# One load queue in the order x, x2, adj, and float32 products for one and a half units, in a two-branch graph layer

## The reference

```python
def _cxin_conv(x, a, eps, W, b):            # N = 4096, D = 128, L = 3
    ax = a @ x
    h = ax + (1.0 + eps[0]) * ax
    for i in range(L):
        h = jax.nn.relu(h @ W[i].T + b[i])
    return h

h = jnp.maximum(_layernorm(x, axis=-1), 0.0)         # eps 1e-05
out1 = _cxin_conv(h,  adj, eps1, W1, b1)
out2 = _cxin_conv(x2, adj, eps2, W2, b2)
return x + jnp.concatenate((out1, out2), axis=1) @ Wm.T + bm
```

## Time and profile before

| | us |
|---|---|
| median of 3 runs | 406.74 (406.16 to 407.13) |
| profiled execution, own time | 406.39 |
| its span | 404.7 |
| PE busy | 400.2 (99%) |
| PEld busy | 325.4 (80%) |
| DVE busy | 219.1 (54%) |
| ACT busy | 219.4 (54%) |
| POOL busy | 30.5 (8%) |
| DMA | 76.21 MB, mean 188 GB/s |

### The profile page before, as it was taken

One profiled execution on the slowest core, in us unless ns is written; L12 is line 12 of the kernel. 1 busy time (PEld: TensorE's weight loads), 2 busy tenths in 40 slices (PEclk: granted clock), 3 DMA queues, 4 the chain that ended last, 5 costly groups with the idle time before them and its releaser, 6 DMA issues.

```text
span 404.7 us, 4822 instructions
## 1 busy us (share of the span) xinstructions
PE 400.2 (99%) x1751; PEld 325.4 (80%) x1751; DVE 219.1 (54%) x258; ACT 219.4 (54%) x259; POOL 30.5 (8%) x35
## 2 busy tenths in 40 slices
PE   8999999999999999999999999999999999999997
PEld 2788888888888888888888888888888888888886
DVE  3998887656464434551645517345373444755223
ACT  4877667657564533555433556334565335766034
POOL 0243332100010000000100001000000000000100
DMA  7997786754636165334574336653175550740100
GB/s 303 420 377 285 296 314 238 244 208 160 232 146 210 44 241 205 109 120 191 186 280 164 122 128 236 230 206 141 67 262 204 207 196 38 275 166 2 52 0 28
DMA packets 14029, 76.21 MB, mean 188 GB/s; under 512 B 1920, under 2 KB 2176, under 8 KB 6080
## 3 DMA queue, kind: packets, MB, share of 16 engines
q1 hardware_dynamic: 12240, 71.18, 46.9%
q0 software_dynamic: 1200, 3.93, 2.9%
q10 hardware_dynamic: 576, 0.92, 0.6%
HBM read 73.93 MB, written 2.10 MB: 188 GB/s over the span
## 4 chain that ended last, share of the span: by engine, by line
PE 97%; DMA 2%; ACTq 0%; DVE 0%; issue 0%; DVEq 0%
PE acc L591 24%; PE acc L588 24%; PE acc L587 24%; PE second_acc L587 3%; PE second_acc L591 3%; PE second_acc L588 3%; PE hidden L588 3%; PE hidden L591 3%; PE hidden L587 3%; PE acc L605 2%; PE second_acc L605 2%; DMA adj_raw<-adj_first 2%; PE second_acc L619 1%; PE merged L588 1%; PE merged L591 1%; PE merged L587 1%
## 5 line engine op out<-in xcount | busy, mean ns | idle before, releaser
L588 PE MATMUL acc<-adj_hi,feat_hi 128*128 128x512 f32 x432 | 168.1, 389 | 0.0
L587 PE MATMUL acc<-adj_hi,feat_lo 128*128 128x512 f32 x432 | 168.1, 389 | 0.0
L591 PE MATMUL acc<-adj_lo,feat_hi 128*128 128x512 f32 x432 | 168.0, 389 | 0.0
L447 DVE TENSOR_TENSOR adj_lo<-adj_raw,adj_hi 128x2048 fp32r<-128x2048 f32 x48 | 108.3, 2289 | 36.7 <-ACT adj_hi L277 35.8
L277 ACT ACTIVATE adj_hi<-adj_raw 128x2048 fp32r<-128x2048 f32 x48 | 90.3, 1925 | 16.5 <-PE acc L591 14.6
L453 DVE TENSOR_TENSOR act_lo<-act_f,act_hi 128x512 fp32r<-128x512 f32 x60 | 41.0, 690 | 105.3 <-ACT act_f L297 105.3
L588 PEld LDWEIGHTS acc<-adj_hi,feat_hi 128*128 128x128 f32 x432 | 81.1, 188 | 17.1
L587 PEld LDWEIGHTS acc<-adj_hi,feat_lo 128*128 128x128 f32 x432 | 81.1, 188 | 17.1
L591 PEld LDWEIGHTS acc<-adj_lo,feat_hi 128*128 128x128 f32 x432 | 81.1, 188 | 16.8
L296 ACT ACTIVATE act_hi<-hidden,bias 128x512 fp32r<-128x512 f32 x45 | 30.9, 687 | 96.2 <-PE hidden L591 96.2
L507 DVE TENSOR_TENSOR adj_lo<-adj_raw,adj_hi 128x2048 fp32r<-128x2048 f32 x14 | 31.5, 2289 | 6.5 <-ACT adj_hi L315 6.2
(11 more groups left out here) (91 smaller groups left out, 251.3 us busy)
## 6 DMA issues: line engine op xcount, KB each, us to landing
adj_raw<-adj_tiles SPq DMA_DIRECT2D x62, 1024.0 KB, 5.1
x_rows<-x_tiles SPq DMA_DIRECT2D x15, 256.0 KB, 7.1
x_res<-x_t POOLq DMA_DIRECT2D x8, 256.0 KB, 6.4
out_t<-y_sb POOLq DMA_DIRECT2D x7, 256.0 KB, 2.3
adj_raw<-adj_second SPq DMA_DIRECT2D x2, 512.0 KB, 6.6
adj_raw<-adj_first ACTq DMA_DIRECT2D x2, 256.0 KB, 5.0
adj_raw<-adj_first SPq DMA_DIRECT2D x2, 256.0 KB, 4.7
w_raw<-w_t SPq DMA_DIRECT2D x1, 512.0 KB, 5.8
```

Of the source, the lines that this page charges most:

```text
L447: nc.vector.tensor_tensor(adj_lo[:, u % RING, :], adj_raw[:, u % RING, :], f32(adj_hi[:, u % RING, :]), ALU.subtract).then_inc(lo_made, 1)
L587: nc.tensor.matmul(out, lhs_lo, rhs_hi, start=start, stop=False)
L588: nc.tensor.matmul(out, lhs_hi, rhs_hi, start=False, stop=False)
L591: return nc.tensor.matmul(out, lhs_hi, rhs_lo, start=False, stop=stop)
```

## The change

- SP's queue issues x, x2, then all pieces of both first units, then the rest as before. ACT issues no loads any more.
- `WARM_UP` is 12 instead of 8.
- `raw_aggregate` is done for the first unit and for the first half of the second. The other half of the second unit goes through three float32r passes in branch 1, at the end of a new `opening_of_second`. The branch-0 products of the two units are now done one unit after the other (`opening_of_first`, `opening_of_second`).
- The sixteen subtractions that make `feat_lo` move from GpSimd to DVE, each to a written-out place in DVE's order. GpSimd's program now begins with its load of `x_res`.
- Epsilon is added in the root as its bias, a constant tile `ln_eps`; the Newton step reads variance and epsilon in one operation. One small DVE operation per tile goes.
- The order of ACT's work in the opening changes with it; the tile of x2 with u = 0 is rounded early, not after the second tile.

```diff
-    WARM_UP = 8
+    WARM_UP = 12
...
-
+            load_x(0)
             load_x2(0)
-            for s, i in ((0, 1), (0, 2), (1, 0), (1, 1)):
+            for s, i in [(s, i) for s in range(len(PIECES)) for i in range(len(PIECES[s]))]:
                 to, piece_of, done = piece_load(s, i)
                 sp.dma_start(to, piece_of).then_inc(done, 16)
...
         @block.gpsimd
         def _(pool):
 
-            def low_of_x2(u):
...
-            low_of_x(0)
-            for u in range(1, U):
-                low_of_x2(u)
-                low_of_x(u)
-                if u == 1:
-                    low_of_x2(0)
             pool.dma_start(x_res[:, :], x_t[:, 0:CW]).then_inc(res_loaded, 16)
...
-                nc.scalar.activation(std[:, :], var_eps[:, :], ACT.Sqrt).then_inc(std_made, 1)
+                nc.scalar.activation(std[:, :], mean_var[:, :, 1], ACT.Sqrt, bias=ln_eps[:, :]).then_inc(std_made, 1)
...
-            for i in (0, 3):
-                if i == 3:
-                    act.dma_start(x_rows[:, 0], x_tiles[0]).then_inc(x_loaded[0], 16)
-                to, piece_of, done = piece_load(0, i)
-                act.dma_start(to, piece_of).then_inc(done, 16)
-            act.wait_ge(zero_made, 1)
+            act.wait_ge(constants_made, 2)
             nc.scalar.activation(root_of_zero[:, :], zero[:, :], ACT.Sqrt)
 
-            for i in range(len(PIECES[0]) - 1):
-                piece_high(0, i)
+            piece_high(0, 0)
             std_of_x(0)
-            piece_high(0, len(PIECES[0]) - 1)
-            piece_high(1, 0)
+            piece_high(0, 1)
+            high_of_x2(0)
             act.wait_ge(rstd_made, 1)
             rectify_half(0, half_relu_made, half_feat1_made)
+            piece_high(0, 2)
+            piece_high(0, 3)
+            rectify_half(1, relu_made, feat1_hi_made)
+            piece_high(1, 0)
             piece_high(1, 1)
-            rectify_half(1, relu_made, feat1_hi_made)
             high_of_x2(1)
-            high_of_half(2, 0)
             std_of_x(1)
-            high_of_half(2, 1)
+            high_of_opening(2)
             high_of_opening(3)
...
-                step(last)
-                nc.vector.tensor_scalar(var_eps[:, :], mean_var[:, :, 1], LN_EPS, None, ALU.add).then_inc(var_made, 1)
+                last.then_inc(var_made, 1)
...
+            def low_of_x2(u):
+                rows = slice(u * JB, (u + 1) * JB)
+                dve.wait_ge(x2_loaded[u % X_SLOTS], 16 * (u // X_SLOTS + 1))
+                dve.wait_ge(feat2_hi_made, u + 1)
+                nc.vector.tensor_tensor(feat_lo[:, 1, rows, :], x2_rows[:, u % X_SLOTS], f32(feat_hi[:, 1, rows, :]),
+                                        ALU.subtract).then_inc(feat2_lo_made, 1)
...
             variances(0)
             scale_and_shift(0)
-            for i in range(2, len(PIECES[0])):
-                piece_low(0, i)
-            for i in range(len(PIECES[1])):
-                piece_low(1, i)
+            piece_low(0, 0)
+            piece_low(0, 1)
+            low_of_x2(0)
+            piece_low(0, 2)
+            piece_low(0, 3)
             variances(1)
+            low_of_x(0)
+            piece_low(1, 0)
+            piece_low(1, 1)
+            low_of_x2(1)
             scale_and_shift(1)
             low_of_opening(2)
             low_of_opening(3)
+            low_of_x(1)
             for u in range(2, U - 2):
                 variances(u)
                 scale_and_shift(u)
+                low_of_x2(u)
                 low_of_opening(2 * u)
                 low_of_opening(2 * u + 1)
+                low_of_x(u)
...
+            def opening_of_first():
+
+                out = opening_bank(0, late)
+                pe.wait_ge(half_feat1_made, 1)
+                pe.wait_ge(fine_hi_made, HALF)
+                passes(out, 0, late, [(feat_hi, adj_hi)], range(HALF), start=True)
+                pe.wait_ge(fine_lo_made, HALF)
+                passes(out, 0, late, [(feat_hi, adj_lo)], range(HALF))
+                pe.wait_ge(feat1_hi_made, 1)
+                pe.wait_ge(hi_made, 1)
+                passes(out, 0, late, [(feat_hi, adj_hi)], range(HALF, JB))
+                pe.wait_ge(lo_made, 1)
+                passes(out, 0, late, [(feat_hi, adj_lo)], range(HALF, JB))
                 pe.wait_ge(feat1_lo_made, 1)
-                for s in range(2):
-                    signal(0, late, passes(opening_bank(s, late), s, late, [(feat_lo, adj_hi)]))
+                signal(0, late, passes(out, 0, late, [(feat_lo, adj_hi)]))
+
+            def opening_of_second():
+
+                halves = range(HALF), range(HALF, JB)
+                out = opening_bank(1, late)
+                pe.wait_ge(fine_hi_made, len(PIECES[0]))
+                passes(out, 1, late, [(feat_hi, adj_hi)], halves[0], start=True)
+                pe.wait_ge(fine_lo_made, len(PIECES[0]))
+                passes(out, 1, late, [(feat_hi, adj_lo)], halves[0])
+                pe.wait_ge(hi_made, 2)
+                passes(out, 1, late, [(feat_hi, adj_hi)], halves[1])
+                passes(out, 1, late, [(feat_lo, adj_hi)])
+                pe.wait_ge(lo_made, 2)
+                passes(out, 1, late, [(feat_hi, adj_lo)], halves[1])
+                pe.wait_ge(feat2_hi_made, 1)
+                pe.wait_ge(feat2_lo_made, 1)
+                signal(0, late, passes(opening_bank(1, first), 1, first,
+                                       [(feat_hi, adj_hi), (feat_lo, adj_hi), (feat_hi, adj_lo)], halves[1]))
...
-            for at in range(len(PIECES)):
-                raw_aggregate(at)
-            norm_aggregate()
+            raw_aggregate(0, range(len(PIECES[0])))
+            raw_aggregate(1, [0])
+            opening_of_first()
+            opening_of_second()
```

More of the change, by code:

```diff
@@ L106, in gnn_layer_kernel @@
         zero = sb("zero", [P, 1])
+        ln_eps = sb("ln_eps", [P, 1])
         act_f = sb("act_f", [P, 2, CW])
@@ L134, in gnn_layer_kernel @@
         fine_lo_made = sem("fine_lo_made")
-        zero_made = sem("zero_made")
+        constants_made = sem("constants_made")
         unit_used = sem("unit_used")
@@ L474, in variances @@
                     last = nc.vector.bn_aggr(mean_var[:, j, :], stats[:, j, :])
-                step(last)
-                nc.vector.tensor_scalar(var_eps[:, :], mean_var[:, :, 1], LN_EPS, None, ALU.add).then_inc(var_made, 1)
+                last.then_inc(var_made, 1)
             def scale_and_shift(u):
                 r0, nt = rstd0[:, :], newton[:, :]
+                dve.wait_ge(var_made, u + 1)
                 dve.wait_ge(std_made, u + 1)
                 step(nc.vector.reciprocal(r0, std[:, :]))
-                step(nc.vector.tensor_tensor(nt, r0, r0, ALU.mult))
-                step(nc.vector.scalar_tensor_tensor(nt, nt, -0.5, var_eps[:, :], ALU.mult, ALU.mult))
+                step(nc.vector.scalar_tensor_tensor(nt, r0, -0.5, r0, ALU.mult, ALU.mult))
+                step(nc.vector.scalar_tensor_tensor(nt, mean_var[:, :, 1], LN_EPS, nt, ALU.add, ALU.mult))
                 step(nc.vector.scalar_tensor_tensor(rstd[:, :], nt, 1.5, r0, ALU.add, ALU.mult))
@@ L508, in low_of_opening, with low_of_x @@
                                         ALU.subtract).then_inc(lo_made, 1)
-            nc.vector.memset(zero[:, :], 0.0).then_inc(zero_made, 1)
-            for i in range(2):
-                piece_low(0, i)
+            def low_of_x2(u):
[4 more added lines that the diff above has]
+                                        ALU.subtract).then_inc(feat2_lo_made, 1)
+            def low_of_x(u):
+                rows = slice(u * JB, (u + 1) * JB)
+                dve.wait_ge(feat1_hi_made, u + 1)
+                dve.wait_ge(relu_made, u + 1)
+                nc.vector.tensor_tensor(feat_lo[:, 0, rows, :], x_rows[:, u % X_SLOTS], f32(feat_hi[:, 0, rows, :]),
+                                        ALU.subtract).then_inc(feat1_lo_made, 1)
+            nc.vector.memset(zero[:, :], 0.0).then_inc(constants_made, 1)
+            nc.vector.memset(ln_eps[:, :], LN_EPS).then_inc(constants_made, 1)
             variances(0)
             scale_and_shift(0)
-            for i in range(2, len(PIECES[0])):
-                piece_low(0, i)
-            for i in range(len(PIECES[1])):
-                piece_low(1, i)
+            piece_low(0, 0)
[3 more added lines that the diff above has]
+            piece_low(0, 3)
             variances(1)
+            low_of_x(0)
+            piece_low(1, 0)
+            piece_low(1, 1)
+            low_of_x2(1)
             scale_and_shift(1)
@@ L598, in opening_bank, with passes, raw_aggregate @@
                 return (second_acc if c else acc)[b]
-            def passes(out, s, b, passes_of, start=False):
+            def passes(out, s, b, passes_of, blocks=range(JB), start=False):
                 u = OPENING[s][0]
                 for k, (feat, adj) in enumerate(passes_of):
-                    for j in range(JB):
+                    for j in blocks:
```

(13 more changed lines are left out.)

29 lines of the change are left out of this document (3 added, 26 removed).

## The result

| | before | changed |
|---|---|---|
| median | 406.45 (406.06 to 407.13, 4 runs) | 408.90 (408.83 to 409.00, 4 runs) |
| ratio | | 1.0062 (95%: 1.0051 to 1.0074) |
| profiled execution | 406.39 | 409.0 |
| span | 404.7 | 407.6 |

The changed kernel is 2.45 us slower; 407.1 was forecast, with a range from 405.9 to 408.1. The page after: span, busy times, chain by engine. GpSimd fell from 30.5 to 8.4 us. TensorE's busy time rose by 1.7 us; the four additional warm-ups are 1.56 of that (4.94 against 3.38).

The account below looks back on a forecast made before the run. The prediction took TensorE's unbroken matmul stream as the bound: profiled 406.39 plus 0.64 in the opening and 0 behind it gives 407.03, stated as 407.1 because a median may lie higher; range 405.9 to 408.1.

Parts of the forecast that it names:

- the point: Start of the first passes of unit 2 on TensorE, 18.18 us before; forecast to move by +0.64 us to 18.82.
- its own signs: Forecast wrong if TensorE waits again after 20 us, feat_lo does not end the stall, or the point leaves 18.1 to 19.6.
- the term behind the point: After the opening: DVE's added subtractions stay covered by TensorE's work, so 0 us is added, some 0.3 if not.
- The term for x_res: Opening loads: GpSimd's x_res load, now first, delays each load behind it by 0.62 us, bounds 0 to 0.62.
- "That the loads now stand in one queue should cost little": Opening loads: merging two queues into SP's costs little, since SP's queue alone moved 419 GB/s in 8.6 to 10.2 us.
- Rival 2: Opening: the single queue fills slowly, everything a further 0.62 us late; the point at 19.44, +1.26, time 407.7; chance 0.17.
- "From 20 us on there is none at all": Kernel before: TensorE has no wait from 20 us on, so a shift of the point passes straight into the time.
- The step that decides: DVE's opening: low_of_x(0) stands behind variances(1), which waits for the second x tile; TensorE stalls 0.75 us, to 13.82.
- TensorE's work: In front of the point: six raw blocks instead of eight and six more float32r matmuls, 0.35 us less work.
- The rule on issuing engines: Opening loads: issuers share 16 DMA engines, so merging queues is free and the early x_res load costs 0.62 us.
- Warm-ups: TensorE's start: twelve end between 5.2 and 6.15 us, before its data at 6.1; cost nothing, up to 0.05 us.
- rival 4: TensorE's opening: clock rises later, two first raw blocks at 1.2 GHz add 1.7 us; +1.6 in all, time 408; chance 0.07.

Follow-up runs that it names:

- Experiments 5: The kernel before with the 32-byte var_eps laid behind zero, so weight tiles start 32 bytes lower and activation tiles stay: 407.56 us, ratio 1.0033.
- 10: The changed kernel with weight and activation tiles at the addresses of before (32-byte pad where var_eps was, ln_eps laid last): 407.87 us.
- experiments 1: The changed kernel, still on one queue, with GpSimd's x_res load held back until the last feat_lo of branch 0 is made: 408.51 us.
- 9: The changed kernel with x_res late and the first loads on two queues (SP: x, first and third piece; ACT: x2, second and fourth): 407.42 us.
- 11: The changed kernel with x_res late and the tiles at the addresses of before, still one queue: 407.03 us, ratio 1.0017.
- experiment 3: The changed kernel with low_of_x(0) ahead of variances(1) on DVE: 408.66 us.
- experiment 12: The changed kernel with x_res late, first loads on two queues, low_of_x(0) and piece_low(1, 0) ahead of variances(1), tiles at old places: 406.61 us, ratio 1.001.
- experiment 6: The kernel before with GpSimd's x_res load issued first, ahead of its subtractions, nothing else changed: 407.57 us.
- experiment 2: The changed kernel with x2 and the second and fourth adjacency piece issued by ACT's queue, x_res still early: 408.70 us.

## Why the prediction was wrong

The sign of the point's shift was right, its size and the total were not. The opening was forecast to lose 0.64 us and lost 1.78 at the point, 1.55 from 24 us on; the stretch behind it was forecast at 0 and lost 1.15. By its own signs the forecast is refuted (the point, 19.95, lies outside 18.1 to 19.6), though its two others held: no wait after 20 us, and feat_lo ends the stall.

- **The step that failed outright is the term behind the point: "So nothing is added: 0".** It was argued from DVE's slack, and that held: no TensorE wait after 20 us. But 1.15 us came from the layout of memory, an effect of deleting a 32-byte tile. The diff showed the deletion; the varying pitch of layer products, from start to start (0.23 to 0.24 against 0.2267 in aggregation) was in the trace before. Experiments 5 and 10 show it from both sides.
- **The term for x_res: 0.62 us was charged, with 0.62 as upper bound.** First piece at 6.97 instead of 6.05, second x tile at 12.88 instead of 11.8. Experiments by medians: changed 408.90, x_res late 408.51, two queues 408.70, both 407.42. Either fault mended alone gives little, 0.39 and 0.20; both together give 1.48, and then the opening of the changed kernel equals that of before. The bound took the bytes at 0.42 MB a us. Measured, x_res's packets held the engines 0.81 us and not 0.62, and SP's 0.28 MB in 4 to 6 us took 53.8% of their time, 3.8 us a MB, against 2.7 in the kernel before (383 GB/s at a share of 1.04). The load was issued at 1.52, not at about 1.0.
- **"That the loads now stand in one queue should cost little", from 419 GB/s in 8.6 to 10.2 us**, failed: that was a queue already deep. Rival 2 named it, with a chance of 0.17, and put a further 0.62 us on top of x_res's; its sign, the second x tile after 12.0, came true. By medians one queue is worth 1.09 once x_res is late (experiments 1 and 9), and 0.77 by experiments 9 and 11 when the layers' 1.15 is taken off. Its point of 19.44 is still short of 19.95.
- **"From 20 us on there is none at all"** misread the kernel before: by the starts of its matmuls it was held 0.23 us between 20 and 24 us. With this the forecast's own numbers give +0.41, not +0.64, so this error made the forecast better by luck.
- **The step that decides, `low_of_x(0)` behind the wait for x**, was right in place and size: stall 0.65 (14.14 to 14.79) against 0.75, ended by feat_lo; experiment 3 removes it.
- **TensorE's work**: 12.87 from first product to point against 12.72; right.
- **The rule on issuing engines.** The Trainium skill, "DMA: Bandwidth & Descriptors", section "Issuing engines are not separate DMA queues", says that loads from different issuers share the same DMA engines and that several issuers save only issue time. The traces agree with the first: with Pool's load early, the other queues moved less. They do not bear out the second for a queue that is first filled. The first piece is issued at 1.92 with one queue and at 1.45 in experiment 9, so one more issue ahead explains 0.47 us, while one queue costs 0.77 to 1.09 by medians; and in experiment 11 the engines were busy and slow, as its two lines show. The measurement decides.
- **Warm-ups** end at 5.97 in the view (within the forecast 5.2 to 6.15) and cover nothing up to 7.09, so here they cost nothing, as forecast. With two queues they do hold TensorE (experiment 12). The clock did not fall in the changed kernel. What rival 4 describes, slow first products worth 1.7 us, did happen in experiment 10, see below.

What stays open: why one queue's packets are slow when it is first filled, why x_res's packets take 1.26 us of the engines' time beside two queues where 0.71 would be usual, by what the places of two operands interact, and why the start of the loads differs so much between executions (first piece at 6.97 in the changed kernel, 7.92 in experiment 10 with the same loads).

## What to carry to other kernels

When a kernel is bound by one stream of matmuls, any edit that adds, removes or resizes a tile can move the start of the tiles laid behind it, and that can be worth as much as the edit itself (here 1.15 us, and 0.6 gained from nothing but padding): compare the matmul pitch per operand pair, and separate the layout from the edit with a dummy tile. And when work is taken from an engine, look at what stood behind it in its program: a load that was harmless at 73 us cost 1.2 us at 1.5 (experiment 6). Last, mend faults together as well as one by one: here either alone gave 0.2 to 0.4 us, both 1.5.

## What the hardware showed that I had not expected

- The start addresses of stationary and moving operands change the pitch of float32r matmuls: with some 180 layer products in it, the same stretch took from 311.39 to 313.23 us, about 0.01 us a product at most. Kernels with the same places agree to 0.01 us over 312 (313.23 or 313.24 in the seven kernels with the weights at 32), and the effect depends on both operands.
- While Pool's 0.26 MB were moving, two hardware queues with work in them got 0.11 MB in 1.5 us (experiment 2).
- In the profiled execution of experiment 10 TensorE idled 2.12 us behind its warm-ups, and the first eight float32 records then took 5.37 us instead of 3.67, three steps between them at 0.85, twice the usual 0.43: the 1.2 GHz level. The granted clock is 0.70 in 8 to 10 us, 0.50 in 10 to 12, and 0.996 over the run. Another execution of it (409.26) has 0.995, the three others 0.999 to 1.0. In the changed kernel, 1.12 us of idling did not do this.

```profile
1.03 4.89 PE L742 MATMUL merged<-const-bfloat16-1.0 128*128 128x512 bf16 x12 [1.03 <-PEq L825]
8.04 5.37 PE L604 MATMUL acc<-adj_raw,x_rows 128*128 128x512 f32 x8 [2.12 <-DMA adj_raw<-adj_first]
```
